# Batch 0 of a four-stage residual kernel: its 512x512 weight transposed before the pooling, in the accumulator banks

## The chip, the cores and the metric

The kernel runs on one core of one Trainium2 chip. The metric is the device time of one execution in microseconds (us), the median over runs; lower is better. The unchanged kernel takes 557.05 us (three runs, 556.64 to 557.39).

## What is computed

x has 8 batches of 1024 tokens with 512 channels. Four residual stages follow each other; per batch an integer token picks the weights of the last two and the mask of the second.

```python
x = x + zX*lap_x(x) + zY*lap_y(x) + zR*x*(1 - x)            # L0: 5-point stencil, reflected at the edges
s = tanh(x @ W1 + b1) @ v                                   # L1: scores, masked softmax over tokens
x = x + softmax(mask(s)) @ x / count
x = x + x @ W[subject].T + b[subject]                       # L2: W is 512x512
z = relu(x @ down[p] + down_b[p]); y = x + z @ up[p] + up_b[p]
x = x + layernorm(y) * g[p] + b[p]                          # L3
```

## The kernel before, in words

All matrix work is in float32. A product that needs W, down or up is split in three: each factor is stored as a rounded part (`...h`) and a rest (`...l`), and `split_product` (L697) issues h·h, h·l and l·h. So each weight has two steps beside its load: ScalarE (ACT) copies it rounded (`round_w` into wth, `round_up` into wuh, `round_v` into vh), and a second engine subtracts to get the rest (`rest_w` into wtl and `rest_v` into vl on VectorE, DVE; `rest_up` into wul and `rest_x2` into x2l on GpSimd, POOL).

The order of every engine's work is written out by hand in four functions per engine: `opening` (batch 0 up to the scores), `first` (rest of batch 0, start of batch 1), `steady(b, n, m, q)` (end of batch b, middle of n, start of m) and `last`. Engines meet at semaphores only, and each engine runs its list in order. The part that matters here:

- **Opening.** L0 of batch 0 goes through TensorE (PE): ACT seeds a bank with the scaled sum of the left and right neighbours (`seed_rows`, from `add_sides` on DVE), PE adds a product with the matrix `sides` and one with `ends` and the edge rows (`sum_rows`, L737 and L741), and DVE finishes (`first_diffuse`, L1410) into x1. The edge rows come by DMA, are scaled on ACT (`scale_edges`) and split on DVE (`split_edges`). `keep_warm` and `fill` are products of zeros (L723, L718). `transpose_x1` (L711) transposes x1 in PSUM, `keep_x1t` copies it, `score_hidden` (L755) and `spread_scores` (L763), `scores_by_row` (L769) give the scores.
- **PSUM.** Eight banks: `ys[0..2]` accumulate the output rows (linear and adapter), five form `front_ps` (`pair_a`, `pair_b`, `cbank`). Batch 0 uses ys for `sum_rows`, and then not until its first `seed`.
- **W.** `transpose_w` (L800) transposes W in 16 blocks of 128x128 into pair_b, cbank and pair_a, after the adapter's down product; the last part waits for `zf_ready`, because `adapter_relu` still reads pair_a. `round_w` and `rest_w` follow. `linear(b, q, t)` multiplies 128 tokens by W: 12 matmuls into a bank seeded by ACT (`seed`).
- **Pooling.** `pool_blocks` (L836), `carry_products`, `carry_sums`, `add_carry` (L1555) on DVE write x2f for four column blocks k; x2f has two halves, so block k waits for `rest_x2` of block k-2. `adapter_down` (L697 into pair_a) needs all four x2l.
- **The next batch's L0** goes without PE: POOL `left_and_right` (L564, needs the block before it finished), ACT `scale_rows` and `centre`, DVE `add_around` (L1401), `times_x` (L1421), `diffuse` (L1428). `diffuse(1, 1, c)` raises l0_done, which `transpose_x1(1, 1, c)` waits for.
- **DMA queues.** SP issues the loads in its own order: `load_rows` (its wu load waits for `wul_ready`), `load_scale`, `load_next(.., 0)`, `load_mask`, `load_linear` (W and down, waits for the transposed W), then the rest of `load_next`.

```python
w_ps = (pair_b, cbank, pair_a[:, 0:D])      # where before transposes W's three parts
def transpose_w(n, part):
    ...
        if hb == 3:
            pe.wait_ge(zf_ready, 4 * n + 4)
```

## Time and profile before

| | |
|---|---|
| median of 3 runs | 557.05 us (556.64 to 557.39) |
| the profiled execution: own time, span | 555.42 us, 553.6 us |
| PE busy | 530.6 us, 96% of the span |
| DVE, ACT, POOL busy | 467.9, 312.3, 311.0 us (85%, 56%, 56%) |
| granted PE clock, mean | 0.992 of full speed |
| DMA | 100.83 MB, mean 182 GB/s |

The span runs from the first to the last instruction of the profiled execution; its own time is 1.8 us longer. Busy shares are sums over the span. PE's busy time is not spread evenly: of the 40 equal slices of 13.8 us, those with a share under nine tenths lie in the first fifth (slices 1, 4 to 6) and in the last slice. A row of the timeline gives the start, the duration, the engine, the line, what is written and read, and in brackets how long the engine sat idle before and who ended it. The chain of waits is followed back from the last instruction: each piece is on the path that set the end.

### The profile page before, as it was taken

To read this page: it belongs to the slowest core of one execution; us is meant where nothing else is said; L and a number is where in the kernel's file an instruction comes from. 1 tells how busy PE (TensorE), PEld (TensorE's weight loads), DVE (VectorE), ACT (ScalarE), POOL (GpSimd) and SP (SyncE) were. 2 spreads that over 40 slices of the span, in tenths; PEclk is the share of its full clock that TensorE was granted. 3 is DMA by queue.
4 is the path that set the end of the run, shared out by engine and by line. 5 is a ranking of instruction groups with operands and counts; after the bars stand their busy time and mean duration, and the time that the engine had idled before them with its cause. 6 is when DMAs were issued, how large, how long until landed. Compare 5 with 4: busy or idle time off the path is not lost.

```text
span 553.6 us, 8994 instructions
## 1 busy us (share of the span) xinstructions
PE 530.6 (96%) x2838; PEld 417.1 (75%) x2838; DVE 467.9 (85%) x1164; ACT 312.3 (56%) x545; POOL 311.0 (56%) x283
## 2 busy tenths in 40 slices
PE   8996789999999999999999999999999999999995
PEld 3565576988688876888778885888778886888783
DVE  6548795999799997999889996999979998787677
ACT  5644663477635774576654775367655676335520
POOL 5156713597266944598275962589355872246241
PEclk9997999999999999999999999999999999999999
DMA  7974665585997579973898659965998847422563
GB/s 249 312 191 76 180 219 171 109 175 103 282 308 163 114 190 318 261 140 102 260 317 189 143 142 313 269 141 106 236 331 194 171 98 212 58 58 57 115 90 120
DMA packets 63942, 100.83 MB, mean 182 GB/s; under 512 B 10894, under 2 KB 16526, under 8 KB 63895
## 3 DMA queue, kind: packets, MB, share of 16 engines
q0 software_dynamic: 16544, 29.90, 33.0%
q1 hardware_dynamic: 38096, 53.54, 30.2%
q10 hardware_dynamic: 9254, 16.81, 8.0%
q8 instruction: 23, 0.38, 0.3%
q14 instruction: 25, 0.20, 0.1%
HBM read 67.43 MB, written 31.98 MB: 180 GB/s over the span
## 4 chain that ended last, share of the span: by engine, by line
PE 84%; DVE 7%; ACT 4%; issue 3%; POOL 1%; DMA 1%; ACTq 0%; DVEq 0%
PE y L697 37%; PE front_ps L755 10%; PE front_ps L836 8%; PE front_ps L697 6%; PE front_ps L778 5%; PE front_ps L711 4%; PE front_ps L763 3%; PE front_ps L769 2%; PE front_ps L800 2%; DVE x2f L1555 2%; ACT zh L1140 2%; DVE pn L1509 1%; PE front_ps L810 1%; PE front_ps L782 1%; PE y L737 1%
## 5 line engine op out<-in xcount | busy, mean ns | idle before, releaser
L583 POOL TENSOR_TENSOR norm<-norm 128x1 f32<-128x1 f32 x64 | 51.3, 801 | 150.5 <-DVE norm L1582 149.7
L697 PE MATMUL y<-wth,x2h 128*128 128x512 f32 x256 | 104.0, 406 | 0.0
L697 PE MATMUL y<-wth,x2l 128*128 128x512 f32 x256 | 100.2, 392 | 0.0
L697 PE MATMUL y<-wtl,x2h 128*128 128x512 f32 x256 | 100.0, 391 | 0.0
L601 POOL TENSOR_TENSOR x2l<-x2f,x2h 128x1024 fp32r<-128x1024 f32 x32 | 76.8, 2400 | 14.6 <-ACT x2h L1017 14.4
L564 POOL TENSOR_TENSOR xd<-xn 128x1024 f32<-128x1024 f32 x28 | 54.7, 1954 | 44.2 <-DVE x L1428 22.7
L1555 DVE SCALAR_TENSOR_TENSOR x2f<-alb,small,front_ps 128x128 f32<-128x128 f32 x256 | 70.7, 344 | 1.7 <-POOL x2l L601 0.4
L836 PEld LDWEIGHTS front_ps<-th_pt,x 128*128 128x128 f32 x512 | 62.0, 190 | 6.9 <-DVE x2f L1555 4.1
L836 PE MATMUL front_ps<-th_pt,x 128*128 128x129 f32 x512 | 64.7, 278 | 2.5 <-DVE x2f L1555 1.0
L590 POOL DMA_DIRECT2D out<-o_sb x58 | 57.1, 1056 | 8.1 <-ACT o_sb L1157 7.1
L1017 ACT ACTIVATE x2h<-x2f 128x1024 fp32r<-128x1024 f32 x32 | 34.0, 1062 | 46.6 <-DVE x2f L1555 46.6
L755 PE MATMUL front_ps<-x1t,w 128*128 128x512 f32 x128 | 57.4, 593 | 0.0
L697 PEld LDWEIGHTS y<-wth,x2l 128*128 128x128 f32 x256 | 48.0, 188 | 10.9
L697 PEld LDWEIGHTS y<-wtl,x2h 128*128 128x128 f32 x256 | 48.2, 188 | 8.9
L697 PEld LDWEIGHTS y<-wth,x2h 128*128 128x128 f32 x256 | 48.2, 188 | 9.0
L1571 DVE BATCH_NORM_STATS2 stats<-y 128x6 f32<-128x512 f32 x64 | 44.4, 694 | 11.4 <-PE y L697 10.8
L1017 ACT ACTIVATE x1t<-front_ps 128x1024 f32<-128x1024 f32 x32 | 31.9, 1022 | 35.0 <-PE front_ps L711 35.0
L1157 ACT ACTIVATE o_sb<-o_sb,norm 128x512 f32<-128x512 f32 x58 | 41.0, 718 | 16.7 <-DVE o_sb L1587 14.7
L550 POOL DMA_DIRECT2D xu<-in_x x49 | 50.0, 1384 | 0.0
L1599 DVE TENSOR_TENSOR x<-y,rest_row 128x512 f32<-128x512 f32 x64 | 43.9, 685 | 4.7 <-PE y L697 2.3
L1587 DVE SCALAR_TENSOR_TENSOR o_sb<-y,mv,g_row 128x512 f32<-128x512 f32 x64 | 47.5, 743 | 0.0
L1017 ACT ACTIVATE y<-start_row 128x512 f32<-128x512 f32 x64 | 37.8, 592 | 11.8 <-DVE o_sb L1587 11.8
(138 smaller groups left out, 1092.3 us busy)
## 6 DMA issues: line engine op xcount, KB each, us to landing
xn<-in_x SPq DMA_DIRECT2D x32, 512.0 KB, 7.7
out<-x ACTq DMA_DIRECT2D x58, 256.0 KB, 4.0
out<-o_sb POOLq DMA_DIRECT2D x58, 256.0 KB, 6.4
xu<-in_x SPq DMA_DIRECT2D x21, 512.0 KB, 7.8
xu<-in_x POOLq DMA_DIRECT2D x21, 512.0 KB, 7.6
wn_wd<-in_L_cond_weight SPq DMA_DIRECT2D x8, 1024.0 KB, 6.6
wn_wd<-in_L_cond_down_w SPq DMA_DIRECT2D x8, 256.0 KB, 6.6
up_row<-in_L_cond_up_b SPq DMA_DIRECT2D x8, 256.0 KB, 4.3
```

The lines of the kernel that those rows point to most:

```text
L550: pool.dma_start(dst, src, accum_op=ALU.add).then_inc(below_added[c], 16)
L564: pool.tensor_tensor(xd[:, c % 2, :, :], xn[:, c, :, 0:D], xn[:, c, :, 2:D + 2], ALU.add).then_inc(pool_a, 1)
L583: pool.tensor_tensor(rstd[:, r:r + 1], ve[:, r:r + 1], minus_half[:, :], ALU.pow).then_inc(rstd_ready, 1)
L590: pool.dma_start(out[bass.ds(b, 1), blk(t), :].rearrange("b p d -> p (b d)"), o_sb[:, t % OB, :], accum_op=ALU.add).then_inc(stored[t % OB ...
L601: pool.tensor_tensor(x2l[q][:, k, :], x2f[:, k % 2, :], x2h[q][:, k, :].bitcast(F32), ALU.subtract).then_inc(x2l_ready, 1)
L697: ins = mm(dst, lhs, rhs, start=first and q == 0, stop=last and q == len(parts) - 1, skip_group_check=True)
L755: ins = mm(hidden_ps[h], w1[:, k, :], x1t[q][:, k, half(h)], start=k == 0, stop=k == KD - 1)
L836: ins = mm(front_ps[:, GROUP_BANK[k % 2][g], o:o + P + 1], x1[q][:, k, j, :], pt[:, j, :], start=True, stop=True)
L1017: return act.activation(dst, src, ACT.Identity)
L1555: ins = dve.scalar_tensor_tensor(out=x2f[:, k % 2, blk(j)], in0=alb[:, blk(j)], scalar=carry(k)[:, j:j + 1], in1=front_ps[:, GROUP_BANK[k ...
L1571: back.mark(dve.bn_stats(stats[:, r, :], bank(b, t)[:, :]))
L1587: dve.scalar_tensor_tensor(out=o_sb[:, t % OB, :], in0=bank(b, t)[:, :], scalar=mv[:, t % OB, 0:1], in1=g_row[:, q, :], op0=ALU.subtract, ...
```

## The change

Batch 0's W is no longer transposed by `transpose_w(0, ..)`. Right after the scores, `transpose_first_w(hb)` transposes one quarter each into ys[0], ys[1], ys[2] and, once DVE has read the first, ys[0] again; `round_first_w` and `rest_first_w` follow each. `clear_banks` then multiplies zeros into the three banks, and the first seeds wait for it. The counts of the W semaphores go from three to four for batch 0 (`w_parts`). `sum_rows(t)` becomes `sum_sides(t)` and `sum_ends(t)`, and the table of scalars is filled by `write_table`, which stands at the head of DVE's opening; `add_sides(0)` comes before `make_ends`. One `keep_warm` moves. `rest_up(0, 0)` goes behind the four `rest_x2` on POOL, and `round_up(1, 1)` on ACT from behind `round_x2` to between two `keep_x1t`. Steady batches keep their order.

```diff
         w_ps = (pair_b, cbank, pair_a[:, 0:D])
+        w0_ps = (ys[0], ys[1], ys[2], ys[0])
+        def w_parts(n):
+            return 3 * n + (1 if n else 0)
...
@@ SP, load_linear @@
-                wait_past(sp, wt_ps, 3 * n)
+                wait_past(sp, wt_ps, w_parts(n))
...
@@ POOL, first @@
                 start_sum(0)
-                rest_up(0, 0)
                 rest_x2(0, 0, 0)
                 rest_x2(0, 0, 1)
                 rest_x2(0, 0, 2)
                 rest_x2(0, 0, 3)
+                rest_up(0, 0)
                 left_and_right(1, 3)
...
@@ PE @@
+                if n == 1 and c == 1:
+                    pe.wait_ge(zf_ready, 4)
...
+            def transpose_first_w(hb):
+                pe.wait_ge(wn_ready, 1)
+                pe.wait_ge(rows_taken, NJ)
+                if hb == 3:
+                    pe.wait_ge(wtl_ready, 1)
+                for ob in range(KD):
+                    ins = pe.transpose(w0_ps[hb][:, blk(ob)], wn[:, ob, blk(hb)], ident[:, :])
+                ins.then_inc(wt_ps, 1)
+            def clear_banks():
+                pe.wait_ge(wtl_ready, 4)
+                for t in range(YB):
+                    ins = mm(ys[t][:, :], ends[0:1, 3, :], zh[0:1, 0:D], start=True, stop=True)
+                ins.then_inc(banks_cleared, 1)
...
@@ PE, opening and first @@
+                fill(ys[0][:, :])
                 keep_warm()
-                fill(ys[0][:, :])
                 spread_scalars()
-                keep_warm()
                 fill(ys[1][:, :])
                 fill(ys[2][:, :])
                 fill(cbank)
-                sum_rows(0)
-                sum_rows(1)
...
+                sum_sides(0)
+                keep_warm()
+                sum_sides(1)
+                sum_ends(0)
...
                 spread_scores(0, 1)
+                transpose_first_w(0)
+                transpose_first_w(1)
                 scores_by_row(0)
+                transpose_first_w(2)
+                block_sums(0)
                 down_through_w(0)
-                block_sums(0)
+                transpose_first_w(3)
                 transpose_p(0, 0)
...
+                clear_banks()
                 adapter_down(0, 0)
-                transpose_w(0, 0)
-                transpose_w(0, 1)
-                transpose_w(0, 2)
+                linear(0, 0, 0)
                 transpose_x1(1, 1, 0)
-                linear(0, 0, 0)
                 transpose_x1(1, 1, 1)
                 linear(0, 0, 1)
...
@@ ACT @@
+            def round_first_w(hb):
+                act.wait_ge(wt_ps, hb + 1)
+                copy(wth[:, hb, :], w0_ps[hb][:, :]).then_inc(wth_ready, 1)
...
                 round_up(0, 0)
+                round_first_w(0)
+                round_first_w(1)
+                round_first_w(2)
...
-                small_exps(0)
                 reflect(1, 0)
                 reflect(1, 1)
+                small_exps(0)
...
                 if NJ * b + t < YB:
-                    act.wait_ge(rows_taken, NJ)
+                    act.wait_ge(banks_cleared, 1)
...
@@ DVE, opening @@
+                write_table()
+                add_sides(0)
                 make_ends()
-                add_sides(0)
                 make_sides()
+                add_sides(1)
                 split_edges()
-                add_sides(1)
...
@@ DVE, first @@
                 carry_sums(0, 2)
+                rest_first_w(3)
                 add_carry(0, 2, 2)
...
                 times_x(1, 1)
-                add_around(1, 2)
                 diffuse(1, 1, 1)
-                rest_w(0, 0)
-                rest_w(0, 1)
+                add_around(1, 2)
+                keep_x3(0, 0)
                 add_around(1, 3)
-                rest_w(0, 2)
                 times_x(1, 2)
+                diffuse(1, 1, 2)
                 rest_z(0, 0)
+                keep_x3(0, 1)
                 times_x(1, 3)
-                keep_x3(0, 0)
-                diffuse(1, 1, 2)
                 diffuse(1, 1, 3)
```

The first place is PE's opening, before the first row sum. `y` and `front_ps` are banks, `pn` is the zero tile, `xn,o_sb` is the product with `sides`, `zl,zh` the one with `ends`. Before:

```order
L723 MATMUL front_ps<-pn 128x512 [waits edges_clear]
L718 MATMUL y<-pn 128x512 [waits edges_clear] x2
L718 MATMUL front_ps<-pn 128x512 [waits edges_clear]
L737 MATMUL y<-xn,o_sb 128x512 [waits sides_made,rows_seeded]
L741 MATMUL y<-zl,zh 128x512 [waits edges_split,ends_ready]
L737 MATMUL y<-xn,o_sb 128x512 [waits rows_seeded]
L741 MATMUL y<-zl,zh 128x512
```

And in the changed kernel:

```order
L731 MATMUL y<-pn 128x512 [waits edges_clear] x2
L731 MATMUL front_ps<-pn 128x512 [waits edges_clear]
L750 MATMUL y<-xn,o_sb 128x512 [waits sides_made,rows_seeded]
L736 MATMUL front_ps<-pn 128x512 [waits edges_clear]
L750 MATMUL y<-xn,o_sb 128x512 [waits rows_seeded]
L757 MATMUL y<-zl,zh 128x512 [waits edges_split,ends_ready]
L750 MATMUL y<-xn,o_sb 128x512 [waits rows_seeded]
L757 MATMUL y<-zl,zh 128x512
```

The second zero product stands between the first and the second row's product with `sides`, and the first product with `ends` comes one product later.

The second place is PE in `first`, from the end of the adapter's down product (`x2l,vh`) to the first product of `linear` (`wth,x2h` into y). Before:

```order
L697 MATMUL front_ps<-x2l,vh 128x512
L800 MATMUL front_ps<-ident,wn_wd 128x128 [waits x2s]
L800 MATMUL front_ps<-ident,wn_wd 128x128 x11
L800 MATMUL front_ps<-ident,wn_wd 128x128 [waits zf_ready]
L800 MATMUL front_ps<-ident,wn_wd 128x128 x3
L711 MATMUL front_ps<-ident,x 128x128 [waits wtl_ready,l0_done]
L711 MATMUL front_ps<-ident,x 128x128 x7
L697 MATMUL y<-wth,x2h 128x512 [waits wtl_ready,y_seeded]
```

And in the changed kernel:

```order
L708 MATMUL front_ps<-x2l,vh 128x512
L708 MATMUL y<-wth,x2h 128x512 [waits wtl_ready,y_seeded]
L708 MATMUL y<-wtl,x2h 128x512
L708 MATMUL y<-wth,x2l 128x512
L708 MATMUL y<-wth,x2h 128x512 [waits wtl_ready]
```

The sixteen transposes and the transpose of the next batch's x are gone from between the two; the latter now follows the twelve products.

The third place is DVE after the last pooled block of batch 0 (`x2f`). `xd,xn` is `times_x`, `xd,table,xu` `add_around`, `xd,xu` `diffuse`, `y,rest_row` `keep_x3`, `x2f,zh` `rest_z`. In the changed kernel:

```order
L1474 TENSOR_TENSOR xd<-xd,xn 128x1024 [waits c_done]
L1481 TENSOR_TENSOR x<-xd,xu 128x2x4x128 [waits own_done]
L1454 SCALAR_TENSOR_TENSOR xu<-xd,table,xu 128x1024 [waits pool_a,scaled_rows]
L1658 TENSOR_TENSOR x<-y,rest_row 128x512 [waits base_stored0,y_ps,rest_ready]
L1454 SCALAR_TENSOR_TENSOR xu<-xd,table,xu 128x1024 [waits pool_a,scaled_rows]
L1474 TENSOR_TENSOR xd<-xd,xn 128x1024 [waits c_done]
L1481 TENSOR_TENSOR x<-xd,xu 128x2x4x128 [waits own_done]
L1621 TENSOR_TENSOR zl<-x2f,zh 128x512 [waits zf_ready]
L1658 TENSOR_TENSOR x<-y,rest_row 128x512 [waits base_stored1,y_ps,rest_ready]
L1474 TENSOR_TENSOR xd<-xd,xn 128x1024 [waits c_done]
L1481 TENSOR_TENSOR x<-xd,xu 128x2x4x128 [waits own_done]
```

Three subtractions for wtl, which stood between these before, are gone, and `keep_x3` of tile 1 has come in.

## Rows read from the trace of the kernel before

**Rows 1.** Busy time by stretch: us, then PE, PEld, DVE, ACT, POOL, PEclk, DMA share, GB/s
```profile
100.00:200.00 100.00, 99.35 (x563) 82.27 (x563) 92.85 (x245) 62.58 (x101) 67.26 (x56) 1.00 0.75 176
```

**Rows 2.** Chain that ended last, around the adapter product and W: start, us, what
```profile
68.56 0.89 PE front_ps L800 x8
...
70.39 0.68 ACT x2f L1138
...
72.35 0.87 PE front_ps L711 x8
73.23 2.78 PE y L697 x12
```

**Rows 3.** Timeline of PE there: start, us, what, [idle before <-releaser]
```profile
64.02 0.50 PE L697 MATMUL front_ps<-x2h,vh 128*128 128x512 f32 x1 [1.86 <-POOL x2l L601]
...
71.70 0.66 PE L800 MATMUL front_ps<-ident,wn_wd 128*128 128x128 f32 x4 [1.83 <-ACT zh L1140]
```

**Rows 4.** Timeline of the opening, all engines
```profile
5.66 1.12 PE L723 MATMUL front_ps<-pn 128*128 128x512 f32 x2
...
6.77 0.68 DVE L1381 CAST zh<-o_sb 64x1024 fp32r<-64x1024 f32 x1
...
7.38 1.21 DVE L1394 TENSOR_TENSOR xd<-xn 128x1024 f32<-128x1024 f32 x1
...
7.63 0.72 ACT L1047 ACTIVATE x<-o_sb,table 32x512 f32<-32x512 f32 x1 [1.76 <-DMA o_sb<-in_x]
...
8.86 0.41 DVE L1375 SCALAR_TENSOR_TENSOR o_sb<-o_sb,table 128x128 f32<-128x128 f32 x1
...
9.68 1.12 PE L737 MATMUL y<-xn,o_sb 128*128 128x512 f32 x2 [0.32 <-ACT y L1062]
```

**Rows 5.** The chain of waits, opening: the first transpose of x1
```profile
15.69 1.02 PE front_ps L711 x8
```

**Rows 6.** Timeline from the scores to the pooling
```profile
38.30 3.74 POOL L564 TENSOR_TENSOR xd<-xn 128x1024 f32<-128x1024 f32 x2 [2.93 <-ACT xn L1017]
...
40.99 1.08 DVE L1494 TENSOR_TENSOR small<-small 128x8 f32<-128x8 f32 x1
...
51.79 0.35 DVE L1531 TENSOR_TENSOR prod<-front_ps,small 128x24 f32<-128x24 f32 x3 [0.70 <-PE front_ps L836]
```

**Rows 7.** Timeline of the pooling, POOL and DVE
```profile
54.32 1.27 POOL L595 TENSOR_TENSOR wul<-wu,wuh 128x512 fp32r<-128x512 f32 x1
...
58.27 2.16 DVE L1555 SCALAR_TENSOR_TENSOR x2f<-alb,small,front_ps 128x128 f32<-128x128 f32 x8 [0.39 <-POOL x2l L601]
...
64.42 2.41 POOL L601 TENSOR_TENSOR x2l<-x2f,x2h 128x1024 fp32r<-128x1024 f32 x1 [0.45 <-ACT x2h L1017]
```

**Rows 8.** Timeline, DVE and POOL at once, batch 0 and a later batch
```profile
66.03 1.88 DVE L1421 TENSOR_TENSOR xd<-xd,xn 128x1024 f32<-128x1024 f32 x1 [2.79 <-ACT xd L1068]
...
74.57 1.22 DVE L1421 TENSOR_TENSOR xd<-xd,xn 128x1024 f32<-128x1024 f32 x1
...
75.70 0.69 DVE L1562 TENSOR_TENSOR zl<-x2f,zh 128x512 fp32r<-128x512 f32 x1
...
76.30 1.22 DVE L1421 TENSOR_TENSOR xd<-xd,xn 128x1024 f32<-128x1024 f32 x1
...
190.52 1.29 DVE L1401 SCALAR_TENSOR_TENSOR xu<-xd,table,xu 128x1024 f32<-128x1024 f32 x1
...
190.68 1.54 POOL L583 TENSOR_TENSOR norm<-norm 128x1 f32<-128x1 f32 x1
```

**Rows 9.** W of the next batch: its DMA (KB each, us to landing), its first reader
```profile
wn_wd<-in_L_cond_weight SPq DMA_DIRECT2D x2, 1024.0 KB, 5.4
...
82.58 0.68 DVE L1439 TENSOR_TENSOR wn_wd<-wn_wd,ident 128x512 f32<-128x512 f32 x1
```

**Rows 10.** PE's longest idle time: the row that ends it, and windows of granted clock
```profile
45.11 2.16 PE L810 MATMUL front_ps<-ident,pn 128*128 128x128 f32 x8 [4.67 <-DVE pn L1509]
...
43.00:44.00 1.00, 0.00 (x0) 0.00 (x0) 0.96 (x4) 1.00 (x2) 1.00 (x4) 0.50 0.16 25
...
49.00:50.00 1.00, 0.30 (x2) 0.31 (x3) 0.96 (x2) 1.00 (x4) 0.00 (x0) 0.69 0.86 145
```

More of the change, by code:

```diff
@@ L264, in build @@
         wth_ready = sem("wth_ready")
+        banks_cleared = sem("banks_cleared")
         wtl_ready = sem("wtl_ready")
@@ L859, in linear @@
                 for k in range(KD):
-                    if t == 0 and k != 1:
-                        pe.wait_ge(wtl_ready, 3 * b + (1, 1, 2, 3)[k])
+                    if t == 0 and (k != 1 or b == 0):
+                        pe.wait_ge(wtl_ready, w_parts(b) + ((1, 1, 2, 3) if b else (1, 2, 3, 4))[k])
                     ins = split_product(y[:, :], (
@@ L888, in opening @@
                 fill(cbank)
-                sum_rows(0)
-                sum_rows(1)
-                sum_rows(2)
-                sum_rows(3)
+                sum_sides(0)
+                keep_warm()
+                sum_sides(1)
+                sum_ends(0)
+                sum_sides(2)
+                sum_ends(1)
+                sum_sides(3)
+                sum_ends(2)
+                sum_ends(3)
                 transpose_x1(0, 0, 0)
-                sum_rows(4)
-                sum_rows(5)
+                sum_sides(4)
+                sum_ends(4)
                 transpose_x1(0, 0, 1)
-                sum_rows(6)
-                sum_rows(7)
+                sum_sides(5)
+                sum_ends(5)
+                sum_sides(6)
+                sum_ends(6)
+                sum_sides(7)
+                sum_ends(7)
                 transpose_x1(0, 0, 2)
@@ L1174, in opening @@
                 square(0)
+                square(1)
+                seed_rows(0)
+                reflect(0, 1)
                 scale_edges()
-                reflect(0, 1)
-                seed_rows(0)
                 reflect(0, 2)
-                square(1)
+                seed_rows(1)
+                seed_rows(2)
                 reflect(0, 3)
-                seed_rows(1)
                 square(2)
-                seed_rows(2)
+                seed_rows(3)
+                square(3)
                 keep_x1t(0, 0, 0)
-                square(3)
-                seed_rows(3)
                 keep_x1t(0, 0, 1)
@@ L1206, in first @@
                 keep_p(0, 1)
-                reflect(1, 3)
                 keep_alpha(0)
+                round_first_w(3)
                 round_x2(0, 0, 0)
-                seed(0, 0)
                 round_x2(0, 0, 1)
@@ L1213, in first @@
                 round_x2(0, 0, 3)
-                round_up(1, 1)
+                scale_rows(1, 2)
                 centre(1, 1)
-                scale_rows(1, 2)
+                reflect(1, 3)
+                seed(0, 0)
+                seed(0, 1)
+                adapter_relu(0, 0)
                 scale_rows(1, 3)
-                adapter_relu(0, 0)
-                round_w(0, 0)
                 adapter_relu(0, 1)
-                round_w(0, 1)
-                round_w(0, 2)
+                seed(0, 2)
                 centre(1, 2)
                 keep_x1t(1, 1, 0)
+                keep_x1t(1, 1, 1)
                 centre(1, 3)
-                seed(0, 1)
-                keep_x1t(1, 1, 1)
+                round_up(1, 1)
                 keep_x1t(1, 1, 2)
                 keep_x1t(1, 1, 3)
-                seed(0, 2)
+                store_base(0, 1)
+                hidden(1, 0)
+                scale(0, 0)
                 seed(0, 3)
-                hidden(1, 0)
-                store_base(0, 1)
                 hidden(1, 1)
-                scale(0, 0)
                 store_base(0, 0)
@@ L1357, in make_table, with write_table, link @@
                                   ALU.add).then_inc(beside_made, 1)
+            def write_table():
+                made = [0]
+                def link(ins):
+                    made[0] += 1
+                    ins.then_inc(dve_setup, 1)
+                    dve.wait_ge(dve_setup, made[0])
                 dve.wait_ge(scalars_ps, 1)
@@ L1520, in rest_w, with rest_first_w @@
                 lo, hi = W_PARTS[part][0], W_PARTS[part][-1] + 1
-                dve.wait_ge(wth_ready, 3 * n + part + 1)
+                dve.wait_ge(wth_ready, w_parts(n) + part + 1)
                 dve.tensor_tensor(wtl[:, lo:hi, :], w_ps[part].rearrange("p (k q) -> p k q", k=hi - lo),
                                   wth[:, lo:hi, :].bitcast(F32), ALU.subtract).then_inc(wtl_ready, 1)
+            def rest_first_w(hb):
+                dve.wait_ge(wth_ready, hb + 1)
+                dve.tensor_tensor(wtl[:, hb, :], w0_ps[hb][:, :], wth[:, hb, :].bitcast(F32),
+                                  ALU.subtract).then_inc(wtl_ready, 1)
             def carry_products(n, k):
@@ L1611, in opening @@
             def opening():
+                write_table()
+                add_sides(0)
                 make_ends()
-                add_sides(0)
                 make_sides()
+                add_sides(1)
                 split_edges()
-                add_sides(1)
+                add_sides(2)
                 first_diffuse(0, 0)
-                add_sides(2)
                 first_diffuse(0, 1)
@@ L1630, in first @@
                 maxima(0)
+                rest_first_w(0)
+                block_weights(0)
+                rest_first_w(1)
+                rest_first_w(2)
+                row_weights(0)
+                probabilities(0, 0)
+                rest_v(0)
                 adapter_bias(0)
-                block_weights(0)
-                row_weights(0)
-                rest_v(0)
-                probabilities(0, 0)
+                add_around(1, 0)
                 probabilities(0, 1)
-                add_around(1, 0)
                 add_around(1, 1)
@@ L1677, in first @@
                 add_identity(1)
-                keep_x3(0, 1)
                 mask_scores(1, 0)
```

43 lines of the change are left out of this document (21 added, 22 removed).

## The prediction

> **What bounds the kernel now.** I first read the busy time by stretch. From 100 us on PE works 99.35 of every 100 us at full clock [rows 1], and the change leaves the steady batches' order alone. So nothing is to be won there, and whatever PE gains or loses before that arrives at the end one for one, as long as the other engines keep up. The place to look is the start, where PE has holes. There I followed the chain of waits, then the timeline of each engine, to see what stands ready and what is late.
>
> The hole the change aims at shows in the chain: after the adapter's down product PE transposes W (from 68.56), the chain leaves PE for ACT's relu at 70.39, and PE's next transpose starts only at 71.70 [rows 2, 3]. The last quarter of W goes into the bank that the relu reads, so PE waits 1.83 us for it. The first product with W starts at 73.23 [rows 2].
>
> **The removal: -3.8 us.** From 68.56 to 72.35, where the transpose of the next batch's x begins, PE does nothing but W's transposes and that wait: 3.79 us [rows 2]. All of it leaves this place. The transpose of x (0.87) only moves behind the products, so it is neutral.
>
> **What the removed work costs where it goes.** The sixteen transposes stand now between the scores and the pooling. There PE sat idle for 4.67 us until 45.11 [rows 10], behind DVE. Half a microsecond per quarter fits into that hole, but the quarters also carry ACT's roundings in front of the exponentials. Two quarters go ahead of scores_by_row and one ahead of block_sums, so ACT reaches the exponentials and the two `reflect` of batch 1 about 0.5 us later, not counting the opening's own delay.
>
> **The opening: +0.7 us, absorbed.** DVE makes the table by 6.77; without the cast (0.68) ahead of it the neighbour sum (1.21) ends at 8.0, then come the cast and `sides` (0.75 for its two instructions, which ended at 9.27 [rows 4] behind both). The same three pieces follow the table as before, so `sides` is ready at 9.4 to 9.5, and the first row sum starts at 9.5 instead of 9.68. Then a product of zeros stands in the way, which took 0.9 (5.66 until the next one at 6.6) [rows 4]. Could it fill a wait? The second row's seed is ready by then, and the split edges, which now follow the second `add_sides`, come at 11.5 while PE reaches them at 12.5. So it is pure cost: +0.9 - 0.2 = +0.7 for the first transpose of x, 15.69 before [rows 5], 16.4 now. The rest of the opening is the same PE work.
>
> Where does this 0.7 go? POOL's two sums started at 38.30, right behind the `reflect`, and ran 3.74 us; DVE's L1494 (8 columns, 1.08 us) stood until they ended [rows 6]. They now start at 38.8 to 38.9, since the `reflect` stands behind three roundings of W, so L1494 lets go at 42.6 and the row weights follow 0.5 later. From there DVE has the same 8.5 us of work up to the first `carry_products`, which before waited 0.70 for PE at 51.79 [rows 6]. PE and ACT do not get later than DVE here: batch 0's two halves of p are now split and the first group of the pooling needs only one. So 0.5 is taken out of a slack of 0.7 and `carry_products` starts at 51.7 to 51.95. I take +0.1. If the slack is not there it is +0.7.
>
> **The pooling: +0.4.** `rest_first_w(3)`, 0.69 like the half-size subtraction in [rows 8], stands in front of the third `add_carry`. That one waited 0.39 anyway for POOL [rows 7]. So +0.3, with its wait +0.4. Every later step is a chain of DVE, ACT, POOL, so the last x2l, 64.42 to 66.83 before [rows 7], ends at 67.2, and the adapter product ends at 68.95. The three clearing products fall into PE's waits between the pooled blocks and cost nothing; if they found no wait it would be 0.7. The first seeds need them and start about 67.3 behind ACT's rounding and `centre`, 1 us ahead of need.
>
> Sum so far: 0.4 - 3.8 = -3.4 at the first product with W, -3.3 with the front's 0.1.
>
> **What is late next: DVE, +0.85.** PE then runs 2.78 + 0.87 + 0.87 + 2.78 + 3.44 + 0.87 us (products, transposes, half of the hidden scores) and wants the last tile of batch 1's x1 at 80.55. DVE lost 2.6 us of subtractions here, yet two meetings with POOL eat it. (1) `rest_up(0, 0)` (1.27 [rows 7]) now follows the last `rest_x2` at once. `times_x` reads two SBUF tensors; at 66.03 it took 1.88 instead of 1.22, standing until POOL's subtraction ended at 66.83 [rows 8], and L1494 stood behind two POOL sums in a row. So it is held until 68.5. (2) `left_and_right(1, 3)` is freed by `diffuse(1, 1, 1)` at the moment when DVE goes on with `add_around(1, 2)`. A tiny POOL instruction that met an `add_around` took 1.54 and ended 0.4 after it [rows 8]. So POOL starts its 1.9 at 72.1 and ends at 74.0, and DVE's next `add_around` waits for that. With starts 1.13 and 0.60 apart as in [rows 8]: `add_around` 74.05, `times_x` 75.25, `diffuse` 76.5, `rest_z` 77.65, `keep_x3` 78.25, `times_x` 78.85, `diffuse` 80.1 to 81.3. PE waits 0.85 at the last transpose. Bounds: 0 if one of the meetings fails, 1.3 without the overlap of neighbours.
>
> The Trainium skill ("GPSIMD Engine Reference", 1. Specifications) says that GpSimd's SBUF interfaces are shared with VectorE, in contention with instructions in a 2-port mode or with two SBUF inputs. By that both meetings cost, and the subtractions for W, with one input in PSUM, are free to run beside POOL; a sum without it would be 0.85 better. The rows above agree.
>
> **SP's queue: 0.** `load_rows(1)` waits for `wul_ready`, now at 68.5 to 69 instead of 55.6. Behind it stand 1.6 MB and then W of batch 1. It is issued at about 73.5, about when it was before, while everything else is 2.5 us earlier. It took 5.4 us to land and was read at 82.58 [rows 9], now about 84. The cover is 3 to 5 us.
>
> **Sum.** +0.1 + 0.4 - 3.8 + 0.85 = -2.45 us, rounded -2.4. The profiled execution's 555.42 becomes 553.0. Its time is 1.63 below the median of the runs, so for the median 557.05 - 2.4 = **554.6 us**. A measurement of this kernel can tell 0.2%, 1.1 us, from no change.
>
> **Rivals.** (a) No meeting of DVE and POOL costs PE anything: -3.3, 553.75. For: DVE had 2.79 idle before `times_x`, and which of two engines gets in first is decided by less than 0.1 us. Against: L1494. Chance 0.2.
>
> (b) DVE becomes the bound of the first batch. It needs no new cost, only the front's 0.7 not absorbed, or one more stall such as L1494's 1.08: each delay of DVE now arrives at the end in full, where before PE's own wait covered it. With +0.6 and one or two stalls of 0.5 to 1 the gain is 0.5 to 1.8: 555.2 to 556.5. For: DVE's work in the stretch before the pooling has no gap left. Against: each step has a row. Chance 0.22.
>
> (c) Slower: PE's clock falls at the new waits. After 4.67 us without work the granted clock fell to 0.50 at 43 us and came back only after 49 [rows 10], about 6.6 us low. There PE was not the bound. The change moves the product of zeros that stood before the fills; PE now waits 1.2 us at 8.3, after another hole at 3.5 to 5.3. If the clock falls there, 6.6 us of dense work take 3.3 more: -2.4 + 3.3, 557.95. The same hole comes again in front of down_through_w, 4.5 us of work that ACT and DVE wait for and that reached full clock before; half of it at half clock is 2.2 more, 560.2. I take 559 for it. It decides once PE's idle time matches what came before 43 us; 1.86 us of idle at 62 left the clock alone [rows 3]. The skill's "TensorE: Matmul & The Clock Gate" (What's actually happening) says "the default state is throttled, and activity releases the throttle". By it the fuller stretch from 38 to 46 would keep the clock up instead, which is off the path. Chance 0.08.
>
> Forecast 0.5. **How the numbers follow:** under 555.95 lie the forecast, (a) and a third of (b): 0.78. Within 1.1 us the rest of (b): 0.13. Slower, above 558.15, lies (c), and 0.01 for a later W: 0.09. The range takes (a) with the opening for free at the low end, 552.9, and (b)'s high end at the other, 556.6.
>
> **What would show it.** The first transpose of x at 16.4. `carry_products` at 51.7 to 52. No W transposes after the adapter product, which ends near 69, and the first product with W right behind. `times_x` of over 2 us at 67.2, a POOL sum of over 3 us at 71, and 0.85 us of PE idle ahead of the last transpose. PE's idle time at 41 to 45 shorter and its clock not at 0.50. If `carry_products` comes at 52.5 or later, or PE waits over 1.5 us for the last tile, (b) is right. A clock under 1.00 before 20 us is (c).

## The result, and the profile after

| | before | changed |
|---|---|---|
| median (lowest to highest) of 22 runs each, us | 557.22 (555.11 to 560.42) | 552.94 (551.15 to 558.17) |
| profiled execution: own time, span, us | 555.42, 553.6 | 554.12, 552.3 |
| mean granted PE clock | 0.992 | 0.986 |
| PE, DVE busy, us | 530.6, 467.9 | 535.8, 468.5 |
| PE busy in 100 to 200 us | 99.35 | 99.41 |

The ratio is 0.9934, interval 0.9912 to 0.9955: the changed kernel is faster by 3.7 us (2.5 to 4.9); the two medians lie 4.3 apart. But its profiled execution is only 1.3 us under that of before, and its PE is busy 5 us longer with less to do. Its runs are spread too: the quickest are spans of 549.1 to 549.8 at a mean clock of 0.993 to 0.997, and three of 552.2 to 552.4 have 0.986, the profiled one among them. That one must be read with the clock beside it. (A few runs of 553 to 556 us that have 0.994 to 0.998 stay unexplained.)

The chain of waits of the changed kernel: start, us, what.

```profile
16.25 1.02 PE front_ps L724 x8
...
65.33 6.05 PE front_ps L708 x18
71.38 2.72 PE y L708 x12
...
95.14 0.12 PE front_ps L806 x2
```

The sixteen transposes of W and the wait for the relu are gone from between the adapter product and the first product with W (65.33 and 71.38; before, [rows 2]). But the eighteen products of the adapter take 6.05 us, where they took 4.54 (64.02 [rows 3] to 68.56 [rows 2]). I use `block_sums` of batch 1 as the gauge from here on, since PE is full behind it; before it stood here:

```profile
96.02 0.12 PE front_ps L790 x2
```

So this execution gained 0.88 us there, no more. The windows say why. Columns: stretch and its length, busy us (instructions) of PE, PEld, DVE, ACT, POOL, then the granted clock, DMA share, GB/s.

```profile
41.00:42.00 1.00, 1.00 (x7) 1.00 (x6) 1.00 (x2) 1.00 (x5) 1.00 (x1) 0.50 0.42 82
...
66.00:67.00 1.00, 1.00 (x4) 0.81 (x3) 0.00 (x0) 1.00 (x2) 1.00 (x1) 0.50 0.00 0
```

In half-microsecond windows the clock stands at 0.50 (1.2 GHz) from 38.0 to 45.0 and from 62.0 to 68.7. Before it was low once, 42.5 to 49.7, where PE had nothing to do until 45.11 and then only transposes, off the chain of waits [rows 10]. What the first fall costs stands in the timeline (start, duration, engine, line, what, and in brackets the idle time before and who ended it):

```profile
39.23 6.57 PE L794 MATMUL front_ps<-wn_wd 128*128 128x128 f32 x32
...
45.84 0.60 ACT L1060 ACTIVATE vh<-front_ps 128x512 fp32r<-128x512 f32 x1 [3.06 <-PE front_ps L794]
...
46.47 0.69 DVE L1532 TENSOR_TENSOR vl<-front_ps,vh 128x512 fp32r<-128x512 f32 x1 [2.25 <-ACT vh L1060]
...
52.97 0.35 DVE L1590 TENSOR_TENSOR prod<-front_ps,small 128x24 f32<-128x24 f32 x3
```

`down_through_w` runs at half clock, vh comes late, DVE stands 2.25 us for it, and the first `carry_products` comes at 52.97 instead of 51.79 [rows 6].

The two meetings of DVE and POOL are both there:

```profile
68.05 2.28 POOL L606 TENSOR_TENSOR wul<-wu,wuh 128x512 fp32r<-128x512 f32 x1
...
69.22 2.19 DVE L1481 TENSOR_TENSOR x<-xd,xu 128x1024 f32<-128x1024 f32 x1
...
71.56 2.80 POOL L575 TENSOR_TENSOR xd<-xn 128x1024 f32<-128x1024 f32 x1 [1.23 <-DVE x L1481]
```

`rest_up` takes 2.28 (1.27 before [rows 7]), `diffuse` beside it 2.19 instead of some 1.22, and the next `left_and_right` 2.80 instead of 1.89. By the times, `times_x` (from 67.84, 1.34 us) came first, `rest_up` stood behind it, and `diffuse` behind `rest_up`. PE, late itself by the slow adapter product, never waited for any of this.

### The profile page after: what moved, and what is told of

It reads as the page before. It is cut to its first block, busy times and chain, and to the rows that moved or that the text cites. A ratio compares the mean times of both kernels' runs of the same rounds, so it can differ in the third digit from the quotient of the medians.

```text
span 552.3 us, 9008 instructions
## 1 busy us (share of the span) xinstructions
PE 535.8 (97%) x2841; PEld 421.3 (76%) x2841; DVE 468.5 (85%) x1165; ACT 312.5 (57%) x546; POOL 312.5 (57%) x283
## 4 chain that ended last, share of the span: by engine, by line
PE 85%; DVE 8%; ACT 3%; issue 3%; POOL 0%; DVEq 0%; ACTq 0%
PE y L708 38%; PE front_ps L771 10%; PE front_ps L869 7%; PE front_ps L708 7%; PE front_ps L794 6%; PE front_ps L724 4%; PE front_ps L779 3%; PE front_ps L785 2%; DVE x2f L1614 2%; PE front_ps L816 2%; ACT zh L1189 2%; DVE pn L1562 1%; PE front_ps L843 1%; PE y L750 1%; PE front_ps L798 1%
```

## The experiments

The theory at the start: the removal is worth its 3.8 us; in runs without a fall of the clock the rest is small; where the clock falls, it gives back up to 3. The rivals: the reordered opening gave part of the gain; or DVE and POOL, not the clock, give some back.

**The changed kernel again**, with a profile of its own.

> The changed kernel again, unedited, beside the three edits that follow. Theory A (the granted clock falls by chance at PE's two thin places, 38 and 62 us, and each fall costs 1 to 3 us): over the runs the times lie in steps, about 551.2 with no fall on the path and 554 with both, and the profile shows half clock in none, one or two of the stretches 38-45 and 62-69 us. Theory B (the clock always falls there, the scatter comes from elsewhere): every profile shows both stretches at half clock. Ratio to the kernel before 0.991 to 0.9955 by both.

552.27 us, ratio 0.9928 (0.989 to 0.9967). This profile had no fall at 38, so the clock does not always fall at both places (theory B is out). A window, then PE's and DVE's timeline and the chain:

```profile
41.00:42.00 1.00, 1.00 (x11) 1.00 (x10) 1.00 (x1) 1.00 (x5) 1.00 (x1) 1.00 0.40 78
```

```profile
39.03 3.82 PE L794 MATMUL front_ps<-wn_wd 128*128 128x128 f32 x32
...
42.38 0.17 DVE L1550 TENSOR_TENSOR small<-small 128x8 f32<-128x8 f32 x1
...
44.82 1.27 DVE L1454 SCALAR_TENSOR_TENSOR xu<-xd,table,xu 128x1024 f32<-128x1024 f32 x1
...
50.65 0.35 DVE L1590 TENSOR_TENSOR prod<-front_ps,small 128x24 f32<-128x24 f32 x3
```

```profile
62.98 5.99 PE front_ps L708 x18
68.97 2.75 PE y L708 x12
...
92.76 0.12 PE front_ps L806 x2
```

At full clock `down_through_w` takes 3.82 and `carry_products` comes at 50.65, 1.1 earlier than before the change and 2.3 earlier than in the first profile. The clock still fell at 64.0, and the adapter product took 5.99. Gauge 92.76, so 3.26 gained. The sum up to the first product with W, each against before: front -1.1, pooling +0.1 (from `carry_products` to the adapter product 12.3, before 12.2), half clock +1.45, removal -3.8; -3.4 together, measured 68.97 - (73.23 - 0.87) = -3.39.

**The clock at 38: `down_through_w` ahead of `block_sums`**, so that PE doesn't stand 1.14 us in front of it.

```diff
-                block_sums(0)
                 down_through_w(0)
+                block_sums(0)
```

> One edit of the changed kernel: down_through_w(0) stands before block_sums(0) again, so PE has no wait for ACT's exponentials ahead of it. Theory A (the wait of 1.1 us at 37.7 lets the clock fall, and the half-clock down_through_w of 6.57 instead of 3.7 us is what made carry_products start at 52.97): full clock until 42, down_through_w 3.7 us, carry_products at 51.9 to 52.3, time 0.5 to 1 us under the changed kernel where its clock fell. Rival (the clock falls anyway, because scores_by_row before it is thin work): half clock from 38 again, down_through_w near 6 us, no gain or 0.3 worse, because block_sums comes 4 us later.

554.5 us, 0.9951 (0.9919 to 0.9984): no gain, against what I had expected. The product ran at full clock (37.53, 3.74 us), but `block_sums` now stood behind it, DVE waited 3.33 us for it, and the row weights came at 44.17 (42.38 in same_again). PE in turn sat idle for 4.07 us, and the clock fell within that, from 45.0 to 51.7. `carry_products` waited 0.52 for PE and came at 53.03, 2.4 later than in same_again: 1.8 of it is the new order, made at full clock, and the rest PE at half clock.

```profile
46.83 1.09 PE L843 MATMUL front_ps<-ident,pn 128*128 128x128 f32 x4 [4.07 <-DVE bz L1570]
```

```profile
50.00:51.00 1.00, 1.00 (x7) 1.00 (x6) 1.00 (x2) 0.48 (x1) 0.00 (x0) 0.50 0.10 12
```

So this run doesn't show that the fall at 38 moves when it is kept away: the edit opened an idle time of its own, nearly as long as the 4.67 us of before [rows 10], and the clock fell in it.

**The clock at 62: dense products in front of the clearing**, eight of 128x512 whose results are cleared away, and both put behind the fourth pooled block.

```diff
+                for _ in range(8):
+                    mm(ys[0][:, :], vh[:, 0, :], wth[:, 0, :], start=True, stop=True)
                 for t in range(YB):
                     ins = mm(ys[t][:, :], ends[0:1, 3, :], zh[0:1, 0:D], start=True, stop=True)
...
+                        if n == 0 and h == 0 and k == 2:
+                            warm_and_clear(8)
...
-                clear_banks()
```

> One edit of the changed kernel: eight full-width products of other data go into ys[0] just before its clearing, and both stand inside adapter_down(0), where PE waits for the third x2l. They are work left idle, not part of the result: the clearing follows. Theory A (the wait at 61 to 65 us lets the clock fall; the adapter product then takes 6.05 instead of 4.5 us on the path): full clock from 60 to 72, adapter product 4.5 us, 1.0 to 1.5 us less than the changed kernel's runs with a fall, and the same as its runs without. Rival (the fall is set earlier, by the pooling's waits): half clock from 62 as before and no gain.

> The two edits above together. Theory A: no half clock on the path in any run, scatter of the runs under 1.5 us, median 551 or lower, ratio to the kernel before 0.989 to 0.991. Rival: as the changed kernel, 0.993.

Alone 551.73 us (6 runs), 0.9893 (0.9851 to 0.9935); with `down_through_w` moved too, 555.38, 0.9964 (0.9926 to 1.0003). The chains, first alone, then both:

```profile
64.47 2.31 PE y L835 x8
66.77 0.89 PE y L837 x3
67.66 4.33 PE front_ps L708 x18
71.98 2.04 PE y L708 x9
```

```profile
63.64 1.81 PE y L835 x8
65.45 0.89 PE y L837 x3
66.34 4.33 PE front_ps L708 x18
70.67 2.73 PE y L708 x12
```

The eighteen adapter products behind them run at full clock, 4.33 us, in both. But the eight and the three in front of them now stand on the chain (3.2 and 2.7 us). In the first profile the clock fell all the same, at 61.9, and came back at 65.3 during the eight: the first product with W comes at 71.98, 0.6 later than in the profile with both falls (71.38). In the second it stayed at 1.00 from 62 to 70, and the product comes at 70.67, 0.7 earlier than in the profile of down_first (71.41, adapter product 6.04). So the fillers lost 0.6 in one profile and won 0.7 in the other. The medians decide nothing: 551.73 can't be told from the changed kernel's, nor 555.38 from the 554.5 of down_first. I had expected 551 or less for both edits together, and that was wrong; they keep down_first's order and its fall at 45 (here 45.4 to 52.2).

**The opening.** First the changed kernel with the old opening, then before with the new one, each with PE's, ACT's and DVE's part.

```diff
-                sum_sides(0)
-                keep_warm()
-                sum_sides(1)
-                sum_ends(0)
+                sum_sides(0)
+                sum_ends(0)
+                sum_sides(1)
...
-                add_sides(0)
                 make_ends()
+                add_sides(0)
```

> The changed kernel with the opening of the kernel before on PE, ACT and DVE (whole row sums, filler ahead of the fills, neighbour sum behind the cast, scale_edges first); W still early. Theory A (the opening costs 0.56 by the trace, first transpose of x at 16.25 instead of 15.69, and most of it reaches carry_products): first transpose at 15.7, carry_products 0.3 to 0.6 earlier than with the new opening (50.73 with the clock up, 52.97 with it down), time 0 to 0.6 us less. Rival (the front has slack, as the prediction had it): carry_products unmoved, no difference. Second rival (without the filler between the sums the clock falls in the opening): a stretch at 0.50 before 25 us, 3 us more.

> The kernel before with the changed kernel's opening alone (split row sums, moved filler, new order on ACT and DVE); W late as before. Theory A: first transpose at 16.25 instead of 15.69, the adapter product 0.0 to 0.6 later than 64.02, time the same as before or up to 0.6 more. Rival (the opening is a gain that the trace of one run hides): ratio under 0.998.

With the old opening 553.2, 0.9927 (0.9898 to 0.9956), as the changed kernel; the new opening alone 557.34, 1.0009 (0.9981 to 1.0037), as before. So the opening gives nothing that can be measured. The profile with the old opening has its first transpose at 16.19, not at the 15.7 that I had expected: DVE's first write into the table of scalars starts at 6.00 there and in the changed kernel (first transpose at 16.25), but at 5.77 in the profile of before. It lies between 5.47 and 6.00 over all profiles, whatever the opening, and the openings are only to be compared with this beside them. With the new opening in before it starts at 5.89 and the first transpose comes at 16.09. The opening passes its delay on, though. PE's timeline of before with the new opening:

```profile
50.08 5.17 PE L839 MATMUL front_ps<-th_pt,x 128*128 128x129 f32 x38 [0.71 <-ACT th_pt L1028]
```

The same row of before the change:

```profile
49.70 3.39 PE L836 MATMUL front_ps<-th_pt,x 128*128 128x129 f32 x28 [0.72 <-ACT th_pt L1017]
```

Everything is 0.38 later, and PE's wait in front of the pooling is as long as it was, for it is a wait for ACT, which stands behind `centre` and so behind DVE. The chain of before shows it (`xd` L1068 is `centre`):

```profile
46.10 1.21 DVE xu L1401
...
47.33 1.24 ACT xd L1068
48.57 1.08 ACT th_pt L1017 x3
```

**Without the product of zeros in the opening.**

```diff
                 sum_sides(0)
-                keep_warm()
                 sum_sides(1)
```

> The changed kernel without the zero product between the first and second row's product with sides. Theory A (it waits for nothing and costs its 0.86): second product at 10.9 instead of 11.77, first transpose of x 0.4 to 0.86 earlier, as far as the seeds allow; time 0.3 to 0.8 us less. Rival (it fills a wait for seeds or edges): first transpose of x at 16.2 again, no gain. Second rival (it holds the clock): 0.50 in the profile before 25 us.

550.98 us (10 runs), 0.9904 (0.9873 to 0.9935). First transpose at 15.04 on the chain, 1.2 earlier, but 0.53 of that is the table of scalars, whose first write starts at 5.47; `nofill_around` and `nofill_up_around` below, where it starts at 6.00 as in the changed kernel, have 15.65. So the product of zeros costs 0.6. The opening's clock stays up. The clock was low for 3.5 us alone (38.5 to 42), the adapter product had full clock, gauge 91.71, 4.3 better than before. Now the two meetings are on the chain. Its pieces, and PE's row at the end:

```profile
66.69 2.21 DVE x L1480
...
69.04 2.82 POOL xd L575
```

```profile
79.28 1.09 PE L724 MATMUL front_ps<-ident,x 128*128 128x128 f32 x8 [0.43 <-DVE x L1480]
```

PE waits 0.43 for the last tile. This is the wait I had forecast, at half its size; with the slower start of the transposes behind it (1.09 for eight), the stretch from the first product with W to the gauge is 0.65 longer than in the changed kernel's profiles.

**`rest_up` back in front of the `rest_x2`** on POOL.

```diff
+                rest_up(0, 0)
                 rest_x2(0, 0, 0)
...
-                rest_up(0, 0)
                 left_and_right(1, 3)
```

> The changed kernel with rest_up(0, 0) ahead of the four rest_x2 on POOL again. Theory A (behind them it meets times_x, both stretched, and holds SP's queue; but PE, late by the clock, waits for neither): times_x of 1.2 and diffuse of 1.2 instead of 1.34 and 2.19, wu of batch 1 issued at 58 instead of 70.5, the last tile of x1 about 1 us earlier, and the time unchanged within 0.4 us, or up to 0.85 less in runs without a fall. Rival (rest_up ahead delays the first x2l, which the order of the change avoids): first rest_x2 0.3 to 1 us later and the time 0.3 to 1 more.

552.37 us, 0.993 (0.9894 to 0.9967). `times_x` 1.36, `diffuse` 1.23: the first meeting is gone, and PE waits for no tile. But POOL reaches the first `rest_x2` later, and this is now the chain:

```profile
54.67 1.27 POOL wul L606
...
64.07 4.54 PE front_ps L708 x18
68.62 1.38 PE y L708 x6
```

Gauge 92.40. From `carry_products` to the adapter product it takes 12.7 us instead of 12.3, so it loses 0.4 in front. What it wins behind shows only against a profile whose adapter product had full clock too, and is in the next group.

**Three orders without the product of zeros:** with `rest_up` in front; with that and `add_around(1, 2)` ahead of `diffuse(1, 1, 1)`, as it was before; with the latter alone.

```diff
-                diffuse(1, 1, 1)
                 add_around(1, 2)
+                diffuse(1, 1, 1)
```

> The changed kernel without the filler product in the opening, and with POOL's rest_up(0, 0) back ahead of the rest_x2. Theory (DVE stands in front of POOL's rest_up, and that is what PE meets once the clock stays up): the last x2l comes no later than 64, times_x and diffuse at 65 to 67 take 1.25 each instead of 2.2, PE has no wait at the last transpose of batch 1's x (0.43 in no_filler), and the median is 550.2 to 550.8 beside 550.98 for no_filler. Rival (rest_up in front delays the first x2l and the adapter product by as much as it saves behind): 550.9 to 551.6, adapter product 0.3 or more later than in no_filler (62.77).

> As nofill_up, and DVE's add_around(1, 2) ahead of diffuse(1, 1, 1), as before the change, so that POOL's left_and_right(1, 3) no longer starts in the middle of an add_around. Theory of the two meetings: POOL's L575 at 69 takes 1.9 instead of 2.8, no wait of PE before batch 1's last transpose, 0 to 0.3 us under nofill_up. Rival (diffuse(1, 1, 1) comes 1.2 later and with it l0_done for PE's second transpose and POOL's start, so the order costs what the meeting did): POOL's L575 starts 1.2 later and ends when it did, time equal to nofill_up within 0.3.

> The changed kernel without the filler, with add_around(1, 2) ahead of diffuse(1, 1, 1) alone; rest_up stays behind the rest_x2. Theory: meeting 1 (times_x or diffuse at 2.2 us beside rest_up) stays, meeting 2 goes; PE's wait at the last transpose between 0 and 0.4, time 550.7 to 551.2. Rival: diffuse starts 1.2 later, the last tile comes later than in no_filler and the wait grows to 0.8 to 1.2: 551.4 to 551.9.

Measured 551.77 (6 runs; 0.9858 to 0.9934), 552.67 (0.9888 to 0.9946) and 550.83 (6 runs; 0.9848 to 0.9951); no_filler had 550.98. The lowest runs of all four are 550.1 to 550.5 and the intervals overlap, so no order is ahead in time; that the medians differ by how often the clock fell is likely, but not shown for each run. I had given `nofill_up` 550.8 at most, and `nofill_up_around` no more than that, and was wrong both times; `nofill_around` came out in my range. The chain of `nofill_up`:

```profile
62.50 6.40 PE front_ps L708 x18
68.90 2.72 PE y L708 x12
```

The adapter product began 0.27 earlier than in no_filler, but `carry_products` had come 0.66 earlier (49.77, without a fall at 38): from there on it was 0.4 later, as the rival had it. It ran at half clock (60.0 to 66.7), which hid what the order saved. The meetings behave as expected: `diffuse` 1.22, and with `add_around` first POOL's sum has its plain length again (of nofill_up, then of nofill_up_around):

```profile
67.76 2.80 POOL L575 TENSOR_TENSOR xd<-xn 128x1024 f32<-128x1024 f32 x1 [2.49 <-DVE x L1480]
```

```profile
70.14 1.89 POOL L575 TENSOR_TENSOR xd<-xn 128x1024 f32<-128x1024 f32 x1 [3.56 <-DVE x L1480]
```

It also starts 1.1 us later, counted from `times_x`, as the rival said. `nofill_around` is the only profile in which the clock never fell below 1.00 between 4 and 75 us, and so the cleanest picture:

```profile
62.38 4.52 PE front_ps L708 x18
66.90 2.74 PE y L708 x12
```

```profile
66.19 2.32 DVE L1453 SCALAR_TENSOR_TENSOR xu<-xd,table,xu 128x1024 f32<-128x1024 f32 x1
...
79.12 1.09 PE L724 MATMUL front_ps<-ident,x 128*128 128x128 f32 x8 [0.69 <-DVE x L1480]
```

The stall beside `rest_up` fell on `add_around` this time, the last tile came 0.69 late (between my 0.4 and the rival's 0.8), and the gauge is 91.55, 4.5 under before.

The clock at 38 and the start of the table drop out if one counts from `carry_products` to the gauge. With the adapter product at full clock this takes 41.3 us in no_filler and 41.5 in nofill_around, which have `rest_up` behind the `rest_x2`, and 41.05 in rest_up_first and 41.04 in nofill_up_around, which have it in front. Before it takes 44.2, in the changed kernel's two profiles, at half clock, 42.2 and 42.1. So `rest_up` in front is 0.2 to 0.5 better here once the clock stays up, by four profiles; the times can't show so little.

**W late again.** The changed kernel with batch 0's W transposed, rounded and subtracted where it was before, without the clearing, the next batch's first transpose of x ahead of the products again; the rest as in the changed kernel, but for two small moves that go with W's place (`scale_rows(1, 3)` on ACT, `keep_x3(0, 0)` on DVE).

```diff
-                transpose_first_w(0)
-                transpose_first_w(1)
                 scores_by_row(0)
...
-                clear_banks()
                 adapter_down(0, 0)
+                transpose_w(0, 0)
+                transpose_w(0, 1)
+                transpose_w(0, 2)
+                transpose_x1(1, 1, 0)
                 linear(0, 0, 0)
...
-                round_first_w(0)
-                round_first_w(1)
-                round_first_w(2)
...
                 reflect(1, 0)
```

> The changed kernel with batch 0's W transposed late as before the change (into pair_b, cbank and pair_a behind the adapter product, three rests on DVE), the opening and all else as in the changed kernel. Theory (the gain is the removed 3.8 us of transposes and wait, and the rest of the change is worth nothing or costs a little): 556.2 to 557.4, that is 3.3 to 4.3 above the changed kernel, with the relu wait of 1.8 back after four rows of transposes. Rival (a share of the gain comes from the reordered opening or from POOL and DVE's new order): 554 to 555.5.

559.95 us, 1.0049 (1.0024 to 1.0074): slower than before, and some 6.4 over the changed kernel, where I had said 3.3 to 4.3. Gauge 99.49. The W part is as before; PE's timeline and, behind it, the chain:

```profile
71.44 1.48 PE L816 MATMUL front_ps<-ident,wn_wd 128*128 128x128 f32 x12
75.02 0.66 PE L816 MATMUL front_ps<-ident,wn_wd 128*128 128x128 f32 x4 [2.10 <-ACT zh L1187]
```

```profile
75.68 0.87 PE front_ps L724 x8
```

Some 4.2 us from 71.44 to 75.68, with a wait of 2.10 where before had 1.83: the removal is worth what the sum said, or a little more. The surplus is elsewhere, in front. DVE and POOL:

```profile
36.95 2.73 DVE L1512 TENSOR_TENSOR small<-mask,small 128x64 f32<-128x64 f32 x1
...
34.89 4.70 POOL L575 TENSOR_TENSOR xd<-xn 128x1024 f32<-128x1024 f32 x2
```

The same two in the changed kernel:

```profile
37.21 0.22 DVE L1515 TENSOR_TENSOR small<-mask,small 128x64 f32<-128x64 f32 x1
...
38.49 3.74 POOL L575 TENSOR_TENSOR xd<-xn 128x1024 f32<-128x1024 f32 x2 [2.46 <-ACT xn L1060]
```

Batch 1's `reflect` stands on ACT ahead of the exponentials in the new order. Without the roundings of W in front of it POOL starts its sums 3.6 us earlier, in the middle of DVE's `maxima`, and an operation of 64 columns stands 2.73 us instead of 0.22. In the changed kernel three roundings hold POOL back until DVE is through. With the clock low in `down_through_w` as well (5.94 us), `carry_products` came at 54.87, 1.9 to 4.2 later than in the changed kernel's two profiles. PE sat idle for 5.17 us in front of `block_sums` here, and the clock fell within that (at 39.5). So this run doesn't isolate the W move alone; it shows it (4.2) plus a front made later by a meeting that the move happens to prevent (2.5) and by this fall, less the 1.5 that the adapter product saves at full clock. Against same_again that is 4.2 in front and 2.6 behind `carry_products`, 6.7 at the gauge.

## Why the prediction was right, and which terms were not

Forecast 554.6 (552.9 to 556.6), measured 552.94: faster, as said, in the range, at its low end. The gain is 3.7 where I had 2.4. The removal, the largest term, was right; that the total came so near is in part luck, since a front that I had 1.2 us too late and falls of the clock that I had at zero pull in opposite directions.

- **The removal, -3.8: right.** No W transpose and no relu wait is left between the adapter product and the first product with W, in any profile; late_w puts 4.2 back.
- **The opening, +0.7 for the first transpose: too much.** 16.25 is near the 16.4 that I had, but 0.23 of it is the later start of the table (6.00 beside 5.77). Counted from that start the new opening costs 0.3, though its product of zeros costs 0.6.
- **The front's sum, +0.1: the mis-sized term.** Measured -1.1 with the clock up and +1.2 with it down. The step that failed is "the row weights follow 0.5 later". POOL's sums started at 38.50, 0.2 later and not 0.5 to 0.6, L1547 (before: L1494) let go at 42.28, and the next step of the row weights followed at once, at 42.38, while before it came at 42.60 after 0.53 of idle time that the profile doesn't explain:

```profile
42.60 0.17 DVE L1497 TENSOR_TENSOR small<-small 128x8 f32<-128x8 f32 x1 [0.53 <-DVE small L1494]
```

  So the row weights are 0.2 earlier. From there DVE is the chain alone, as I had it, with 8.3 us instead of 8.5, and before's 0.70 of waiting for PE is gone: `add_around` and then `centre` come forward past four of the eight multiplications of p, so ACT copies the pooling's operands sooner (in same_again `add_around` starts at 44.82, before at 46.02 on). In the order of before this 0.70 was no slack, for there PE was late because ACT was, and ACT because DVE was (before with the new opening passes its 0.38 on whole); the reordered front is what made it one. This comes from the timelines: no run takes the reordering of `first` out by itself. It goes further than the section on the change says: PE's first pooling blocks and, behind `linear`, the adapter's up products stand in a new order too.
- **The pooling, +0.4: too much, 0.1** in both profiles (12.3 and 12.4 us from `carry_products` to the adapter product, 12.2 before). The clearing cost nothing on the path, as said.
- **DVE's two meetings, +0.85: right where the adapter product has full clock.** Both are in both profiles of the changed kernel, with 2.2 and 2.8 us, but the first fell on `diffuse`, not on `times_x`. PE's wait was 0 there, because the half-clock adapter product made PE late by 1.5 itself. In the two profiles without the product of zeros and with that product at full clock the wait was 0.43 and 0.69, and the stretch from the first product with W to the gauge is 0.65 and 0.9 longer. The two costs don't add; the larger one counts.
- **Rival (c), the clock: chance too low, places half right.** I gave it 0.08 and tied it to PE's long idle times. (The hole that it counts at 3.5 to 5.3 us isn't in the trace; PE works there on a product of zeros.) The opening never fell in any profile. `down_through_w` did, in seven of the ten profiles that have it behind `block_sums`, and the adapter product, in whole or in part, in six of the eleven without W's transposes behind it. Three falls do lie in a long idle time, of 5.17 us in late_w, 4.07 in down_first and 4.06 in both_edits (4.67 before). The others don't: what stands ahead of them are short waits (1.14 us at 37.7; 0.69 at 59.5, and 1.86 in front of the adapter product in same_again), single-column products and single-row products. Priced one by one: 1.5 us at the adapter, up to 2.3 at `down_through_w`. The forecast had them at zero.
- **SP's queue, 0: right.** W of batch 1 was issued at 74.4 and 72.1 in the two profiles, landed 7.3 and 6.6 us later, and was first read at 86.20 and 83.83, 4.5 and 5.2 later still.
- **Steady batches untouched: right,** 99.41 of 100 us.

From `carry_products` on I had +0.4 - 3.8 + 0.85 = -2.55. no_filler and nofill_around, with the adapter product at full clock, measure -2.95 and -2.7 there; the changed kernel's own profiles, at half clock, -2.1 and -2.1. An estimate for the changed kernel without any fall is then -1.1 in front and -2.7 to -2.95 behind, 3.8 to 4.1 gained; none of its profiles shows it. The first profile had +1.2 in front and gained 0.9, the second gained 3.3.

The Trainium skill ("TensorE: Matmul & The Clock Gate", What's actually happening) says that activity releases the throttle; I had drawn from it that the fuller stretch from 38 to 46 would keep the clock up. The window above shows PE busy for all of 41 to 42 at 0.50, and the same code at 1.00 in the next profile. The sentence I had made of it fails here. What decides between the two executions no run shows. The Trainium skill ("GPSIMD Engine Reference", 1. Specifications) says that VectorE instructions with two SBUF inputs contend with GpSimd for its SBUF interfaces. The trace agrees in every meeting named here: the DVE operations that stood have two SBUF inputs, and two subtractions for W, with one input in PSUM, took 1.28 us together beside POOL's sum in the first profile.

## What to carry to other kernels

A wait that is seen on one engine is slack only if its releaser isn't itself behind the engine that you are about to delay: follow it back two steps before writing "absorbed", in the new order and not only in the old one. Where two engines share a way into SBUF, an edit on a third (three roundings on ACT) can decide whether they meet; list, for each long POOL operation, the DVE operations that fall into it before and after. Where a median moves less than the sum says, look at windows of the clock before looking for a wait. Where an edit meant for one thing changes the result, look first at what else came later by it: down_first lost 1.8 us by its order before its clock fell. And compare two profiles by stretches with common ends, since their starts alone differ by up to half a microsecond.

## What the runs showed of the hardware

- The same program falls to half clock at a place in one execution and not in the next (38 us: 0.50 in the first profile of the changed kernel, 1.00 in the second). The steps are 3.4 to 7 us long, and a fall costs between nothing (before, where PE is off the chain) and 2.3 us.
- A DVE operation of 64 columns (0.22 us) stood 2.73 us beside two POOL sums in a row, from 36.95, in the middle of the first, until both had ended (39.59). How long it stands is set by POOL's operations, not by DVE's. POOL's side pays as well: 1.89 became 2.80.
- The clock fell after single-column products and a wait of 1.14 us in six of nine profiles that have both, and stayed up in three. It also fell within each of the idle times of over 4 us in this stretch (4.67 us before, 4.07 in down_first, 4.06 in both_edits, 5.17 in late_w).
